# GpSimd's waits for free slots of gathered rows, moved from TensorE's products to the next step of ScalarE and VectorE, in a four-layer graph network

## The chip, the cores and the metric

The kernel runs on one core of a Trainium2 chip (trn2). The metric is the device time of one execution in microseconds (us): lower is better. The engines are TensorE (PE in the profile), VectorE (DVE), ScalarE (ACT), GpSimd (POOL) and SyncE (SP).

## The reference

A graph has 12,500 nodes of 64 features and 212,500 edges, sorted by their target node. Four layers run one after the other. Each normalizes the node features, makes a message for each edge from the row of its source node, adds the messages up by target and adds the result to the node features:

```python
# layer 0: softmax aggregation, feature by feature
m = relu(feats[src] + edge_h) + EPS
ex = exp(m - segment_max(m, dst)[dst]);  a = ex / segment_sum(ex, dst)[dst]
h = segment_sum(m * a, dst)              # then a norm, two matrix products and a batch norm
# layer 1: mean
agg = segment_sum(x[src], dst) / max(degree, 1);  out = concat([agg, x]) @ W.T + b
# layer 2: hyperbolic attention; u = -hh[row], v = hh[col] on the Poincare ball
ma = (coef1[:, None] * u + coef2[:, None] * v) / den[:, None]
e = -2.0 / sqrt_c0 * arctanh(clip(sqrt_c0 * norm(ma), 1e-08, CLIP))
att_log_h = segment_sum(softmax_over_row(e)[:, None] * log_h[col], row)
# layer 3: relational attention, 8 relations, 4 heads
s = leaky_relu(el[edge_rel, src] + er[edge_rel, dst]);  w = softmax_over_dst(s)
h = segment_sum(feat_all[edge_rel, src] * w[..., None], dst) + h_bias
```

## The kernel before

The program goes through nine stages. Each layer has one long loop over its edges, and a shorter stage follows each loop, in which the nodes are updated. The loops are `softmax_edges(0)`, `mean_edges`, `hyperbolic_edges` and `softmax_edges(3)`; the change touches only these.

**Steps and slots.** A softmax or mean loop has `STEPS` = 208 steps, each of two streams (`HALVES`) of `W` = 512 edges, in `TILES` = 4 tiles of 128. The hyperbolic loop has `CHB` = 230 steps of `BT` = 8 tiles of 128 edges. In each of the four loops GpSimd fetches the source rows of a step with eight indirect DMAs, one for each tile: lines 648 (both softmax loops), 955 (mean) and 1172 (hyperbolic). Rows land in a buffer of `SLOTS` = 4 slots (`rows`, in the profile `rows` or `m_rows`; `rows_d`, in the profile `h_rows_d`), so the gathers of step c overwrite the rows of step c - 4.

**The wait.** `slot_free(eng, sem, c, each, ago)` makes an engine wait until `sem` has reached `c * each + (1 - ago) * each`, that is until the step c - `ago` has been counted there; `each` is the number of increments in a step. It is nothing for the first `ago` steps:

```python
def slot_free(eng, sem, c, each=1, ago=2):
    if not (isinstance(c, int) and c < ago):
        eng.wait_ge(sem, c * each + (1 - ago) * each)
```

**Stages of a step.** Each engine executes its own list of stages, in program order. A stage with lag n works on the step that is n behind the newest one. The order of the lists sets the order of the work; no scheduler changes it.

- Softmax, layer 0. TensorE: `to_columns` (lag 0) turns the gathered rows and adds the edge features, in the product of line 765, whose last instruction increments `turned` (here `rows_read` is the same semaphore); then `count` (1) and `to_rows` (2). ScalarE: `move` (0, line 823, increments `moved`), `exps` (1, lines 827 and 828), `copy_out` (2, line 835), and a store. VectorE: bins (line 666), `segment_sums` (2), maxima (1, lines 698 to 706). SyncE's load of `attr` waits for `rows_read` too (line 614) and isn't changed.
- Softmax, layer 3. TensorE: `v_columns` (0), `score_columns` (1; line 787 increments `turned`), `to_rows` (3). ScalarE: `widen` (0), `move` (1, line 821, increments `moved`; it also waits until VectorE has bent the step before), then as above. VectorE: `own_values` (0, line 675), sums, maxima.
- Mean. TensorE: `to_columns` (line 966 increments `turned`), `to_rows` (line 973) and the products of line 985. VectorE's scan `segment_sums` (line 1048) waits for `turned` and increments `summed`. ScalarE copies out in line 1001.
- Hyperbolic. TensorE: `add_up` (3, line 1192, increments `multiplied`), `expand` (1, line 1210), `turn_hot` (0, line 1201, increments `turned`). ScalarE: square (2, line 1225), root, weigh, `move` (0, line 1234, waits for `turned`, increments `moved`). VectorE: `differ` (2), `messages` (3), `compare` (0), `distances` and `ratios` (2), and last `runs` (3, line 1338), eight operations of a chain that wait for `multiplied` and increment `ran` eight times in a step. In VectorE's turn `runs` stands behind `distances` and `ratios`, which need ScalarE's square and root.

Each of the later events is reached only when the earlier one has been, since `move`, `segment_sums` and `runs` wait for it.

Of the kernel before, what the change touches and what calls it, by code (L numbers as in the profile page):

```python
# [31 lines left out]
SLOTS = 4  # L32
# [15 lines left out]
BT = 8  # L48
# [28 lines left out]
def build(nc, x, src, dst, edge_attr, edge_type, w0a, b0a, gamma, beta, w0b, b0b, scale0,  # L77
          w1, b1, w2, c2, w3, al3, ar3, b3, out):
    with ExitStack() as whole:
# [30 lines left out]
        def counter(names, ctx):  # L110
            return [nc.alloc_semaphore(name=n) for n in names.split()]
# [274 lines left out]
        with nc.cleanup_on_exit(), ExitStack() as ctx:  # L386
# [8 lines left out]
            named, ran, prev_in, prev_out, normed, put, upto_ready, var_ready, std_ready = counter(  # L395
                "named ran prev_in prev_out normed put upto_ready var_ready std_ready", ctx)
# [126 lines left out]
# [4 lines that stand above are left out]
# [8 lines left out]
        def softmax_edges(layer):  # L535
# [6 lines left out]
            with nc.cleanup_on_exit(), ExitStack() as ctx:  # L542
# [6 lines left out]
                def sem(name):  # L549
                    return nc.alloc_semaphore(name=f"{name}_{layer}")  # L550
# [28 lines left out]
                if rel:  # L579
# [5 lines left out]
                    weighed, summed, back, copied, issue, pe_turn, got_b, parted, powered, merged, m_step, put_cross = (  # L585
                        sem(n) for n in (
                            "seeded v_turned v_spread v_own widened turned masked moved bent carried topped lowered diffed exped "
                            "weighed summed back copied issue pe_turn got_b parted powered merged m_step put_cross").split())
                scan_out = scan3 if rel else scan0
                ROWS = 16 * HALVES * TILES  # L590
                rows_read = turned
                END = (STEPS - 1) % 2

                with nc.Block() as block:
# [46 lines left out]
                    @block.gpsimd  # L641
                    def _(pool):
                        for c in range(STEPS):
                            b = c % SLOTS
                            slot_free(pool, rows_read, c, ago=SLOTS)
                            for k in range(TILES):
                                for h in range(HALVES):
                                    pool.indirect_dma_start(  # L648
                                        out=rows[:, b, k, h * GW:(h + 1) * GW], out_offset=None,
                                        in_=table3s.rearrange("n (q f) -> (n q) f", f=HEADS) if rel else table0,  # L650
                                        in_offset=bass.IndirectOffsetOnAxis(ap=idx_all[:, h, c, k:k + 1], axis=0)) \
                                        .then_inc(got_rows[b], 16)
# [199 lines left out]
        def mean_edges():  # L852

            with nc.cleanup_on_exit(), ExitStack() as ctx:
# [6 lines left out]
                def sem(name):  # L861
                    return nc.alloc_semaphore(name=f"m_{name}")
# [27 lines left out]
                seeded, turned, summed, back, copied, issue, blank, cleared, got_b, merged, put_cross = (sem(n) for n in (  # L890
                    "seeded turned summed back copied issue blank cleared got_b merged put_cross").split())
# [26 lines left out]
                with nc.Block() as block:  # L918
                    @block.sync
                    def _(sp):  # L920
                        def load(c, b, r):
                            slot_free(sp, summed, c, ago=SLOTS)
                            sp.sem_inc(issue, 1)
                            for h in range(HALVES):
                                sp.dma_start(same_b[h * D:(h + 1) * D, b, :],
                                             row(same, c + h * STEPS).broadcast_to([D, W])).then_inc(got_mask[b], 16)

                        def store(c, b, r):
                            sp.wait_ge(copied, c + 1)
                            sp.sem_inc(issue, 1)  # L930
                            for h in range(HALVES):
                                sp.dma_start(edge_rows(scan1, c + h * STEPS), out_e[:, b, h, :, :]).then_inc(put[b], 16)

                        steps(sp, STEPS, (0, load), (3, store))
                        for b in range(SLOTS):
                            sp.wait_ge(put[b], 32 * (STEPS // SLOTS))
                        last_b = sp.value_load(cross_i[0:1, 0:1], min_val=HALF, max_val=EP - 1)
                        sp.dma_start(state_b[:, 0:1], scan1[bass.ds(last_b, 1), :].rearrange("a f -> f a"),
                                     allow_slow_non_contiguous=True).then_inc(got_b, 16)
                        sp.wait_ge(merged, 1)  # L940
                        sp.dma_start(scan1[bass.ds(last_b, 1), :].rearrange("a f -> f a"), joined[:, 0:1],
                                     allow_slow_non_contiguous=True).then_inc(put_cross, 16)
                        sp.wait_ge(put_cross, 16)

                    @block.gpsimd
                    def _(pool):
                        pool.iota(columns[:, :], pattern=[[1, SORTED]], base=0, channel_multiplier=0,
                                  allow_small_or_imprecise_dtypes=True).then_inc(named, 1)

                        for c in range(STEPS):  # L950
                            b = c % SLOTS
                            slot_free(pool, turned, c, ago=SLOTS)
                            for k in range(TILES):
                                for h in range(HALVES):
                                    pool.indirect_dma_start(  # L955
                                        out=rows[:, b, k, h * D:(h + 1) * D], out_offset=None, in_=table1,
                                        in_offset=bass.IndirectOffsetOnAxis(ap=idx_all[:, h, c, k:k + 1], axis=0)) \
                                        .then_inc(got_rows[b], 16)
# [137 lines left out]
        def hyperbolic_edges(c_col, inv_sqrt_c):  # L1096

            with nc.cleanup_on_exit(), ExitStack() as ctx:
# [6 lines left out]
                def sem(name):  # L1105
                    return nc.alloc_semaphore(name=f"h_{name}")
# [26 lines left out]
                    weighed, messaged, multiplied, ran, u_step, c_turn, d_step, r_step, l_step, issue, issue_a, pe_turn = (sem(n) for n in (  # L1133
                        "upright got_map placed spread cleared split compared turned moved expanded apart squared spaced rooted bounded "
                        "weighed messaged multiplied ran u_step c_turn d_step r_step l_step issue issue_a pe_turn").split())
# [8 lines left out]
                with nc.Block() as block:  # L1144
                    @block.sync
                    def _(sp):
                        sp.dma_start(block_s[:, :], block_g.rearrange("(a n) -> a n", a=1)).then_inc(got_map, 16)
                        sp.dma_start(goes_on[:, :], goes_g.rearrange("(a n) -> a n", a=1).broadcast_to([P, NT])).then_inc(got_map, 16)
                        sp.wait_ge(got_map, 32)

                        def load_blocks(c, b, r):
                            slot_free(sp, expanded, c, ago=SLOTS)
                            sp.sem_inc(issue, 1)
                            _, blocks = nc.values_load_multi_w_load_instructions(
                                block_s[0:1, bass.ds(c * BT, BT)], engines=(mybir.EngineType.SP,), min_val=0, max_val=BLOCKS - 1)
                            for k, at in enumerate(blocks):
                                sp.dma_start(near[:, b, k, :], table2[bass.ds(at * P, P), 0:D + 1]).then_inc(got_near[b], 16)

                        steps(sp, CHB, (0, load_blocks))

                    @block.gpsimd
                    def _(pool):
                        pool.iota(place[:, :], pattern=[[1, P]], base=1, channel_multiplier=0,
                                  allow_small_or_imprecise_dtypes=True).then_inc(placed, 1)

                        for c in range(CHB):
                            b = c % SLOTS
                            if c * BT in (0, 8 * P):
                                pool.wait_ge(u_step, 3 + 3 * (c > 0))
                            slot_free(pool, multiplied, c, ago=SLOTS)  # L1170
                            for k in range(BT):
                                pool.indirect_dma_start(  # L1172
                                    out=rows_d[:, b, k, :], out_offset=None, in_=table2,
                                    in_offset=bass.IndirectOffsetOnAxis(ap=idx_d[:, c * BT + k:c * BT + k + 1], axis=0)).then_inc(got_rows[b], 16)
# [1033 lines left out]
```

## Time and profile before

| | |
|---|---|
| three runs | 12235.75, 12268.7 (median), 12348.68 us |
| the profiled execution | 12218.17 us, its span 12216.4 us |
| loop of layer 0 / mean / hyperbolic / layer 3 | 2507 / 2499 / 3152 / 2446 us |
| busy over the span: PE, DVE, ACT, POOL | 6560.5, 6951.0, 4184.0, 7235.6 us |

No engine is busy for more than 59% of the span. In the rows below, a line of a timeline has the start of an instruction (or of several merged, then with their number behind an x), its duration, its engine and line of the kernel, what it writes and reads, and in brackets how long the engine was idle just before it and what is thought to have ended that. The name behind such an arrow is inferred; where it names a DMA that landed long before, it was something else.

### The profile page before, as it was taken

What the parts mean: (1) busy time and instruction counts of PE and PEld (TensorE: products, weight loads), DVE (VectorE), ACT (ScalarE), POOL (GpSimd) and SP (SyncE); (2) the same over time, 40 slices, a digit from 0 to 9 for tenths busy, and PEclk for the clock granted to TensorE, in tenths of its full rate; (3) what the DMA queues carried; (4) which work ended last, traced back from release to release, by engine and by line L of the source; (5) the groups of instructions that cost most, each with busy time, mean ns of one, the idle gap of its engine ahead of it and who ended that gap; (6) DMA issues with size and microseconds to landing.
All of it is one profiled execution on the core that took longest, in us unless ns stands there. A gap on an engine that the chain in (4) does not pass through costs nothing. (4 is left out here: it accounts for less than half of the span.)

```text
span 12216.4 us, 120473 instructions
## 1 busy us (share of the span) xinstructions
PE 6560.5 (54%) x28159; PEld 5236.5 (43%) x28159; DVE 6951.0 (57%) x14143; ACT 4184.0 (34%) x8456; POOL 7235.6 (59%) x7482
## 2 busy tenths in 40 slices
PE   0655555553155555552356666666665555555552
PEld 0333333332145555551356666666664333333331
DVE  3556555667355555541645555555555477777775
ACT  0222222222055555551134444444444322222221
POOL 5666666664656666666155555555554666666665
PEclk9666666665577777775555555555556666666665
DMA  4333333332422222222033333333334444444442
GB/s 89 108 110 109 111 110 107 111 109 47 134 54 56 56 55 56 55 56 27 12 85 78 78 78 79 79 77 79 77 78 114 117 114 114 113 114 115 114 114 78
DMA packets 1318230, 1059.32 MB, mean 87 GB/s; under 512 B 815857, under 2 KB 1034376, under 8 KB 1316531
## 3 DMA queue, kind: packets, MB, share of 16 engines
q0 software_dynamic: 238720, 318.69, 13.9%
q1 hardware_dynamic: 681698, 373.56, 12.0%
q10 hardware_dynamic: 397397, 362.35, 9.1%
q8 instruction: 161, 2.64, 0.1%
q14 instruction: 254, 2.08, 0.1%
HBM read 580.99 MB, written 472.73 MB: 86 GB/s over the span
## 5 line engine op out<-in xcount | busy, mean ns | idle before, releaser
L1172 POOL DMA_INDIRECT h_rows_d<-table,h_idx_d x1840 | 1750.6, 951 | 1389.1 <-PE h_ps_sum L1192 812.6
L648 POOL DMA_INDIRECT rows<-table,idx_all x1664 | 1643.0, 987 | 870.8 <-issue 476.0
L955 POOL DMA_INDIRECT m_rows<-table,idx_all x1664 | 1575.0, 947 | 911.0 <-issue 453.2
L648 POOL DMA_INDIRECT rows<-table3s,idx_all x1664 | 1574.4, 946 | 872.5 <-issue 476.0
L985 PE MATMUL m_ps_sort<-m_hot_high,m_hot_low 128*128 128x224 f32 x3328 | 1056.9, 497 | 973.6 <-issue 818.2
L985 PEld LDWEIGHTS m_ps_sort<-m_hot_high,m_hot_low 128*128 128x128 f32 x3328 | 920.2, 283 | 1081.5 <-issue 941.0
L795 PE MATMUL ps_out<-ident,sums 128*128 128x128 f32 x3328 | 776.7, 398 | 965.6 <-issue 690.5
L1192 PE MATMUL h_ps_sum<-h_rows_d,h_hot 128*128 128x65 f32 x3680 | 832.0, 417 | 635.6 <-DVE h_rows_d L1329 352.1
L795 PEld LDWEIGHTS ps_out<-ident,sums 128*128 128x128 f32 x3328 | 629.9, 221 | 1131.5 <-issue 1075.6
L1192 PEld LDWEIGHTS h_ps_sum<-h_rows_d,h_hot 128*128 128x128 f32 x3680 | 795.4, 328 | 719.9 <-issue 719.9
L1210 PE MATMUL h_ps_src<-h_near,h_hot_t 128*128 128x65 f32 x3680 | 838.2, 419 | 462.1 <-DMA h_near<-table 252.8
L1210 PEld LDWEIGHTS h_ps_src<-h_near,h_hot_t 128*128 128x128 f32 x3680 | 803.1, 331 | 494.2 <-issue 493.6
L1048 DVE TENSOR_TENSOR_SCAN m_sums<-m_same_b,m_sums,m_ps_rows 128x512 f32<-128x512 bf16 x208 | 266.2, 1280 | 1078.5 <-issue 900.4
L835 ACT ACTIVATE out_e<-ps_out 128x512 f32<-128x512 f32 x832 | 446.3, 590 | 1049.3 <-remote 711.3
L1234 ACT ACTIVATE h_hot_t<-h_ps_hot 128x1024 f32<-128x1024 f32 x230 | 235.8, 1025 | 1566.2 <-DMA at_first<-m_zeros 1480.5
L666 DVE TENSOR_TENSOR hot<-bins,cat 128x784 bf16<-128x784 bf16 x208 | 202.8, 976 | 937.9 <-DMA rows_p<-dst_i,dest 847.1
L763 PE MATMUL ps_score<-ident,rows 128*128 128x128 f32 x1664 | 547.9, 423 | 305.4 <-issue 254.8
L1023 ACT ACTIVATE m_hot_low<-m_hot_low,record,m_slope 128x128 f32<-128x128 f32 x1664 | 663.8, 486 | 6.1
L1338 DVE SCALAR_TENSOR_TENSOR h_run<-h_run,h_goes_on,h_ps_sum 128x65 f32<-128x65 f32 x1840 | 519.2, 282 | 240.2 <-PE h_ps_sum L1192 6.2
L1087 DVE SCALAR_TENSOR_TENSOR m_junk<-cat,m_ps_base 128x98 f32<-128x98 f32 (+61 forms) x1664 | 594.2, 423 | 98.1 <-issue 50.6
L821 ACT ACTIVATE score_c<-ps_score 128x512 f32<-128x512 f32 x208 | 124.4, 598 | 1480.7 <-DMA table<-Hn 1196.5
L675 DVE TENSOR_TENSOR_SCAN spread_v<-marks,spread_v,ps_v 64x512 f32<-64x512 bf16 x208 | 263.7, 1268 | 635.9 <-issue 635.9
(425 smaller groups left out, 14233.0 us busy)
## 6 DMA issues: line engine op xcount, KB each, us to landing
scan<-out_e ACTq DMA_DIRECT2D x832, 256.0 KB
h_near<-table SPq DMA_DIRECT2D x1840, 32.5 KB
run_g<-h_run ACTq DMA_DIRECT2D x230, 260.0 KB
part_b<-part SPq DMA_DIRECT2D x832, 64.0 KB
max_b<-top ACTq DMA_DIRECT2D x416, 128.0 KB
scan<-m_out_e SPq DMA_DIRECT2D x416, 128.0 KB
attr<-in_edge_attr SPq DMA_DIRECT2D x415, 128.0 KB
h_rows_d<-table,h_idx_d POOLq DMA_INDIRECT x1840
```

The lines of the kernel that those rows point to most:

```text
L648: pool.indirect_dma_start(out=rows[:, b, k, h * GW:(h + 1) * GW], out_offset=None, in_=table3s.rearrange("n (q f) -> (n q) f", f=HEADS) if ...
L763: nc.tensor.matmul(ps_score[:, b % 2, k::TILES], rows[:, b, k, :], ident[:, :], start=True, stop=False)
L795: mm = nc.tensor.transpose(ps_out[:, j, k * P:(k + 1) * P], sums[:, b % 2, j, k::TILES], ident[:, :])
L835: ins = a.activation(out_e[:, b, :, :, j * D:(j + 1) * D], ps_out[:, j, :].rearrange("p (k h f) -> p h k f", k=TILES, h=HALVES), ACT.Copy)
L955: pool.indirect_dma_start(out=rows[:, b, k, h * D:(h + 1) * D], out_offset=None, in_=table1, in_offset=bass.IndirectOffsetOnAxis(ap=idx_al ...
L985: nc.tensor.matmul(ps_sort[:, 0:SORTED], hot_low[:, w % 2, j, :], hot_high[:, w % 2, j, :], start=n == 0, stop=n == PC - 1).then_inc(place ...
L1023: ins = a.activation(hot_low[:, w % 2, j, :], hot_low[:, w % 2, j, :], ACT.Relu, bias=record[:, at:at + 1], scale=slope[:, at:at + 1])
L1087: v.scalar_tensor_tensor(junk[:, at % 4, 0:BLOCKS + n], cat[:, p, 0:BLOCKS + n], cat[:, p, BLOCKS + n:BLOCKS + n + 1], ps_base[:, 0:BLOCKS ...
L1172: pool.indirect_dma_start(out=rows_d[:, b, k, :], out_offset=None, in_=table2, in_offset=bass.IndirectOffsetOnAxis(ap=idx_d[:, c * BT + k: ...
L1192: mm = nc.tensor.matmul(ps_sum[:, k // HB, (k % HB) * ACC2:(k % HB + 1) * ACC2], hot[:, b, k, :], rows_d[:, b, k, D + 1:ROW2], start=True, ...
L1210: mm = nc.tensor.matmul(ps_src[:, k // HB, (k % HB) * (D + 1):(k % HB + 1) * (D + 1)], hot_t[:, b % 2, k * P:(k + 1) * P], near[:, b, k, : ...
L1338: v.scalar_tensor_tensor(run[:, b, k, :], before, goes_on[:, bass.ds(c * BT + k, 1)], ps_sum[:, k // HB, (k % HB) * ACC2:(k % HB + 1) * AC ...
```

## The change

In each loop GpSimd's `slot_free` names another semaphore: in both softmax loops `moved` (ScalarE, lines 821 and 823) for `rows_read` (TensorE), in the mean loop `summed` (VectorE, line 1048) for `turned` (TensorE), in the hyperbolic loop `ran` (VectorE, line 1338, eight increments a step) for `multiplied` (TensorE). All are still four steps back. No instruction is added, removed or moved on any engine; the three lines below are all of it.

```diff
@@ softmax_edges, GpSimd @@
                             b = c % SLOTS
-                            slot_free(pool, rows_read, c, ago=SLOTS)
+                            slot_free(pool, moved, c, ago=SLOTS)
                             for k in range(TILES):
@@ mean_edges, GpSimd @@
                             b = c % SLOTS
-                            slot_free(pool, turned, c, ago=SLOTS)
+                            slot_free(pool, summed, c, ago=SLOTS)
                             for k in range(TILES):
@@ hyperbolic_edges, GpSimd @@
                                 pool.wait_ge(u_step, 3 + 3 * (c > 0))
-                            slot_free(pool, multiplied, c, ago=SLOTS)
+                            slot_free(pool, ran, c, each=BT, ago=SLOTS)
                             for k in range(BT):
```

## Rows read from the trace of the kernel before

**Rows 1.** Windows of the four loops: stretch and length, busy us (instructions), clock, DMA, GB/s

```profile
233.00:2740.00 2507.00, 1435.45 (x7018) 909.56 (x7019) 1464.85 (x1853) 545.45 (x1028) 1643.00 (x1664) 0.65 0.38 108
...
3046.00:5545.00 2499.00, 1259.84 (x4934) 1134.46 (x4934) 1261.11 (x3777) 1267.92 (x3520) 1575.34 (x1665) 0.74 0.26 66
...
6138.00:9290.00 3152.00, 2052.45 (x9184) 1936.06 (x9184) 1659.26 (x5280) 1412.33 (x1839) 1750.64 (x1840) 0.51 0.39 78
...
9564.00:12010.00 2446.00, 1376.87 (x5359) 944.84 (x5360) 1795.11 (x2260) 674.17 (x1441) 1574.41 (x1664) 0.64 0.41 112
```

**Rows 2.** Waits of GpSimd over the span: us in total, times, longest us

```profile
POOL h_rows_d L1172 <- PE h_ps_sum L1192: 812.6, 192, 11.8
...
POOL rows L648 <- DMA table<-Hn: 384.7, 102, 6.7
POOL rows L648 <- remote: 373.9, 102, 6.4
POOL m_rows L955 <- DMA rows<-table,idx_all: 293.3, 129, 10.3
...
POOL m_rows L955 <- PE m_ps_rows L966: 164.4, 58, 19.0
```

**Rows 3.** Timeline of the layer 0 loop, two steps

```profile
986.07 1.60 POOL L648 DMA_INDIRECT rows<-table,idx_all  x1 [3.64 <-remote]
...
998.95 0.44 PE L765 MATMUL ps_score<-ident,attr 128*64 128x128 f32 x4
...
1005.49 0.95 POOL L648 DMA_INDIRECT rows<-table,idx_all  x1 [0.30 <-issue]
...
1009.73 0.58 ACT L823 ACTIVATE ps_score<-ps_score 128x512 f32<-128x512 f32 x1 [2.62 <-remote]
...
1009.96 1.60 POOL L648 DMA_INDIRECT rows<-table,idx_all  x1 [3.53 <-remote]
```

**Rows 4.** Timeline of the layer 3 loop, the end of a batch of gathers

```profile
10507.42 0.95 POOL L648 DMA_INDIRECT rows<-table3s,idx_all  x1 [0.30 <-issue]
...
10512.01 0.60 ACT L821 ACTIVATE score_c<-ps_score 128x512 f32<-128x512 f32 x1 [11.77 <-DMA table<-Hn]
```

**Rows 5.** Timeline of the start of the layer 0 loop

```profile
282.68 0.95 POOL L648 DMA_INDIRECT rows<-table,idx_all  x1 [0.31 <-issue]
289.80 0.58 ACT L823 ACTIVATE ps_score<-ps_score 128x512 f32<-128x512 f32 x1 [24.10 <-remote]
```

**Rows 6.** Timeline of the stage behind the mean loop, ScalarE

```profile
5678.43 0.59 ACT L1427 ACTIVATE lin_rows_t<-lin_ps_t 128x500 f32<-128x500 f32 x1 [33.01 <-DMA m_same_b<-same]
```

**Rows 7.** Timeline of the mean loop, the end of a batch of gathers

```profile
4006.34 0.96 POOL L955 DMA_INDIRECT m_rows<-table,idx_all  x1 [0.30 <-issue]
...
4006.83 0.60 PE L966 MATMUL m_ps_rows<-ident,m_rows 128*128 128x128 f32 x4
...
4009.10 1.28 DVE L1048 TENSOR_TENSOR_SCAN m_sums<-m_same_b,m_sums,m_ps_rows 128x512 f32<-128x512 bf16 x1 [5.60 <-issue]
...
4009.28 0.95 POOL L955 DMA_INDIRECT m_rows<-table,idx_all  x1 [1.98 <-DMA rows<-table,idx_all]
```

**Rows 8.** Timeline of the hyperbolic loop, one step

```profile
7505.67 0.95 POOL L1172 DMA_INDIRECT h_rows_d<-table,h_idx_d  x1 [3.35 <-PE h_ps_sum L1192]
...
7508.82 3.19 DVE L1338 SCALAR_TENSOR_TENSOR h_run<-h_run,h_goes_on,h_ps_sum 128x65 f32<-128x65 f32 x8
...
7509.10 1.91 PE L1201 MATMUL h_ps_hot<-ident,h_hot 128*128 128x128 f32 x8
...
7513.54 3.65 PE L1192 MATMUL h_ps_sum<-h_rows_d,h_hot 128*128 128x65 f32 x16 [2.52 <-issue]
7514.43 0.95 POOL L1172 DMA_INDIRECT h_rows_d<-table,h_idx_d  x1 [0.30 <-issue]
7517.19 1.02 ACT L1234 ACTIVATE h_hot_t<-h_ps_hot 128x1024 f32<-128x1024 f32 x1 [6.51 <-DMA at_first<-m_zeros]
...
7517.60 0.95 POOL L1172 DMA_INDIRECT h_rows_d<-table,h_idx_d  x1 [2.22 <-PE h_ps_sum L1192]
...
7522.01 3.19 DVE L1338 SCALAR_TENSOR_TENSOR h_run<-h_run,h_goes_on,h_ps_sum 128x65 f32<-128x65 f32 x8
```

## The prediction, made before the changed kernel ran

> **What bounds the kernel now.** I first read the stage windows. In none of the four loops is an engine full: GpSimd, the busiest or nearly so, gathers for 1643 of 2507 us in layer 0, 1575 of 2499 in the mean loop, 1751 of 3152 in the hyperbolic one and 1574 of 2446 in layer 3 [rows 1]. A step takes 2507 / 208 = 12.05 us, 2499 / 208 = 12.01, 3152 / 230 = 13.70 and 2446 / 208 = 11.76. Eight gathers of 0.95 us with 0.30 us between them [rows 3] take 9.7 us of it. What is left is the time in which GpSimd waits for its slot, so these few microseconds are what the change works on. GpSimd's waits show them: 192 of 812.6 us in all before line 1172, 102 + 102 of 3.7 us before line 648 (every second step), 129 + 58 before line 955 [rows 2].
>
> Next I read timelines around such waits, for what GpSimd waits for and when it really was ready. Here is the odd thing. In layer 0 TensorE ends the last product of a step at 999.39, yet ScalarE's `move`, which waits for it, starts only at 1009.73, just when GpSimd starts again too, 3.3 us after the gather that ended at 1006.44 [rows 3]. In the mean loop the last gather ends at 4007.30, TensorE's product at 4007.43, and VectorE's scan and GpSimd both start at 4009.1 to 4009.3 [rows 7]. In the hyperbolic loop TensorE's `turn_hot` is over at 7511.01, the gathers at 7515.38, and ScalarE's `move` starts at 7517.19, GpSimd at 7517.60 [rows 8]. So work that TensorE has long finished reaches its waiters a fixed time behind the end of a batch of gathers: 1.8 us behind 8 gathers [rows 7, 8], 3.3 to 3.6 behind 16 [rows 3, 4], 6.2 behind the opening 40 [rows 5]. It grows with the batch. Behind the mean loop, where GpSimd issues 212 indirect DMAs and waits for none of TensorE's semaphores, ScalarE waits 33 us for a product [rows 6]: the gathers hold the news back, not GpSimd's own wait.
>
> The Trainium skill, Perfetto Trace Analysis, in "Tensor Engine Instruction", has the semaphore update pushed when PSUM acknowledges the last bytes, with no part in it for GpSimd. By that alone ScalarE would have started 10 us earlier in layer 0; the trace does not agree.
>
> What bounds a loop is then the cycle batch of gathers, hold, restart of GpSimd. Whatever delays the restart delays the next batch, its end, and the next release.
>
> **The change, part by part.** It adds no instruction. Queued behind the wait on GpSimd are only the gathers of this step and all later ones; TensorE (or ScalarE in layer 3) waits for these rows. SyncE's queue is passed by nothing, and its waits stay.
>
> *Do the rows come too late?* Between the release of step c - 4 and the use of step c lie about three periods, 36 us in the softmax and mean loops and 41 in the hyperbolic one; the gathers take 9.7 us. Some 24 us are spare, by this estimate. The added waits are 0.6, 1.3 and 6 to 8 us (below), so the rows still come in time and this costs nothing. The cover is thin only early in the mean loop, where GpSimd once waits 19.0 us [rows 2]: I allow 0 to 25 us for it and take 10.
>
> *Softmax, both layers.* At 1009.73 ScalarE starts `move`, and GpSimd now waits for its end, 0.58 us later, instead of starting at 1009.96. In layer 3 it is 0.60 us [rows 3, 4]. The wait bites once in two steps, 102 times a layer: 0.6 x 102 = 61 us in each, 122 us in all. Lower bound: 0, if the release of TensorE's news doesn't hang on the restart. Upper bound: every step pays, 0.6 x 208 x 2 = 250 us. I take 122, since the second step's `move` is done long before its eight gathers' turn.
>
> *Mean.* GpSimd starts 0.18 us after the scan has started; now it needs the scan's end, 1.28 us [rows 7]. 187 waits [rows 2] x 1.28 = 239 us. Bounds: 0 and 1.28 x 208 = 266. With the 10 us above: 249.
>
> *Hyperbolic.* This is the large unknown. Of the step whose `multiplied` lets GpSimd start at 7505.67, `runs` ends at 7512.01, 6.3 us later; of the next, at 7525.20 against 7517.60, 7.6 us later [rows 8]. If nothing overlapped, 6.5 x 226 = +1469 us would be the upper bound. But most of this lateness is VectorE standing behind `ratios`, work that goes on beside the gathers; with a later batch more of it is done when the release comes. What can't overlap is gathers 9.71, hold 1.81, the eight runs 3.19, restart 0.17: 14.88 us a step against 13.70. That is +1.18 x 226 = +267 us. Lower bound: the next two batches starting at 7505.67 and 7517.60 are 11.93 us apart [rows 8], which is a step whose wait is short; if the later start brought every step there, (11.93 - 13.70) x 230 = -407 us. I take +267, as it is the sum of the parts that stand in series in the trace.
>
> **Sum.** 122 + 249 + 267 = +638 us on the profiled execution's 12218.17: 12,856, forecast 12,850 us. That execution is 50.5 us (0.4%) under the median of 12268.7; against the median the forecast is +4.7%.
>
> **The rivals.**
>
> *Faster (opposite side).* The hold isn't uniform: `multiplied` of the product that ended at 7505.40 reached GpSimd at 7505.67, when no batch was running, and the later one of 7517.19 at 7517.60 [rows 8]. If the later restart puts TensorE's products into the pause between batches, their news comes at once, ScalarE and VectorE no longer wait for the end of a batch, and the chain gets shorter than the batch it waits for. For it speaks that GpSimd is idle more and the other engines are held less; against it, that a pause is only as long as the chain it waits for, and add_up (3.65 us) and the runs follow each other. It decides where `multiplied` is counted before the hold sets in. At the lower bound of the hyperbolic loop and no cost elsewhere: 12218 - 407 = 11,811; if the other loops still pay their 371, 12,182, within the measure of no change. Chance of a clear gain 0.13.
>
> *No change.* The news of TensorE is released by something that does not hang on when GpSimd restarts, and the spare 24 us swallow all. Then 12,218 to 12,243. For it: rows are fetched early. Against: three waiters on three engines start within 0.3 us of GpSimd [rows 3, 7, 8]. Chance 0.20, with the mixed case at 12,182. The rule of the Trainium skill quoted above (Perfetto Trace Analysis) belongs to this rival, since by it nothing ties a product's news to the gathers.
>
> *Only the small terms.* Hyperbolic breaks even, the rest pays: 12218 + 371 = 12,589. Chance 0.19.
>
> *No overlap.* The hyperbolic loop pays its lateness in every step, wholly or in large part: 12218 + 371 + 1469 = 14,058 at most, 13,200 if a third is paid. Chance 0.08.
>
> *It doesn't do what it says:* the new waits are reached before the old ones. It can't be, as each new event follows its old one.
>
> **How the numbers follow.** The forecast's own case has 0.40 and runs from 12,650 to 13,050 (softmax at 0 to 250, mean 239 to 291, hyperbolic 200 to 400). The range leaves out most of the clear gain and most of the no-overlap case, and holds the rest: 12,180 to 13,180. A measurement of this kernel can tell about 1%, 123 us, from no change: faster (under 12,146) 0.13, same 0.20, slower (over 12,391) 0.67, which is 0.40 + 0.19 + 0.08.
>
> **What the profile of after would show.** In layer 0, GpSimd's waits before line 648 go from 3.7 to 4.3 us, still every second step, and the loop from 2507 to about 2568 us. In the mean loop VectorE's scan still starts 1.8 us behind the last gather, GpSimd 1.3 to 1.5 us behind the scan, the loop takes about 2750. In the hyperbolic loop GpSimd waits 5.2 us before line 1172, nearly always for line 1338, and the loop takes about 3420 us. Gathers stay at 0.95 us, and the short stages stay as they are. I am wrong about the cycle if GpSimd's restart comes later and the loops don't get longer; wrong about the hold if the scan of the mean loop starts less than 1 us behind TensorE's product while gathers run; wrong about the overlap if line 1338 starts long after `multiplied` is counted.

## The result, and the profile after

The changed kernel takes 12838.78 us (median of three runs, 12832.34 to 12845.94) against 12268.7: ratio 1.0465, 95% interval 1.0433 to 1.0498. The forecast was 12,850. Its profiled execution took 12832.34 us, 614.2 more than that of before; the sum had said 638.

Where the time went is read from the page's costliest groups: line, engine, operation, count, busy us and mean ns of one, then the idle us just before them and what ended it. Busy and idle time of the gathers of one line together are the length of that loop's stream of gathers (with the idle time before its first gather). Before:

```profile
L1172 POOL DMA_INDIRECT h_rows_d<-table,h_idx_d x1840 | 1750.6, 951 | 1389.1 <-PE h_ps_sum L1192 812.6 <-issue 494.4 <-remote 73.3
L648 POOL DMA_INDIRECT rows<-table,idx_all x1664 | 1643.0, 987 | 870.8 <-issue 476.0 <-remote 373.9 <-POOLq L386 20.8
L955 POOL DMA_INDIRECT m_rows<-table,idx_all x1664 | 1575.0, 947 | 911.0 <-issue 453.2 <-DMA rows<-table,idx_all 293.3 <-PE m_ps_rows L966 164.4
L648 POOL DMA_INDIRECT rows<-table3s,idx_all x1664 | 1574.4, 946 | 872.5 <-issue 476.0 <-DMA table<-Hn 384.7 <-POOLq L1979 11.9
```

After:

```profile
L1172 POOL DMA_INDIRECT h_rows_d<-table,h_idx_d x1840 | 1747.1, 949 | 1762.7 <-DVE h_run L1338 1230.5 <-issue 524.1 <-DVE h_loc L1286 8.0
L955 POOL DMA_INDIRECT m_rows<-table,idx_all x1664 | 1575.8, 947 | 1072.6 <-DVE m_sums L1048 578.5 <-issue 473.3 <-DMA rows<-table,idx_all 20.8
L648 POOL DMA_INDIRECT rows<-table,idx_all x1664 | 1611.8, 969 | 945.1 <-issue 554.9 <-ACT ps_score L823 369.4 <-POOLq L386 20.8
L648 POOL DMA_INDIRECT rows<-table3s,idx_all x1664 | 1578.2, 948 | 904.8 <-issue 475.9 <-ACT score_c L821 417.0 <-POOLq L1979 11.9
```

| loop | stream before | after | difference | term of the sum |
|---|---|---|---|---|
| layer 0 | 2513.8 | 2556.9 | +43 | +61 |
| mean | 2486.0 | 2648.4 | +162 | +249 |
| hyperbolic | 3139.7 | 3509.8 | +370 | +267 |
| layer 3 | 2446.9 | 2483.0 | +36 | +61 |

The four differences are 611 of the 614 us. GpSimd's waits, which answer to [rows 2], now name the new semaphores' engines (us in total, times, longest us):

```profile
POOL h_rows_d L1172 <- DVE h_run L1338: 1230.5, 163, 15.8
...
POOL m_rows L955 <- DVE m_sums L1048: 578.5, 166, 7.4
...
POOL rows L648 <- ACT score_c L821: 417.0, 102, 6.8
POOL rows L648 <- ACT ps_score L823: 369.4, 85, 7.5
```

These rows don't hold every stop, since some are put down to other names. Counted in the two traces as gaps of over 0.4 us ahead of the first gather of a step, the stops are:

| loop | stops before | sum, us | stops after | sum, us |
|---|---|---|---|---|
| layer 0 | 102 | 373.9 | 147 | 460.3 |
| mean | 188 | 458.6 | 188 | 620.4 |
| hyperbolic | 226 | 885.8 | 179 | 1246.0 |
| layer 3 | 102 | 384.7 | 102 | 417.0 |

The timeline of the mean loop answers to [rows 7]: last gather, then TensorE's news, VectorE's scan, GpSimd.

```profile
4507.32 0.60 PE L966 MATMUL m_ps_rows<-ident,m_rows 128*128 128x128 f32 x4
...
4509.05 0.95 POOL L955 DMA_INDIRECT m_rows<-table,idx_all  x1 [0.30 <-issue]
4511.84 1.28 DVE L1048 TENSOR_TENSOR_SCAN m_sums<-m_same_b,m_sums,m_ps_rows 128x512 f32<-128x512 bf16 x1 [6.23 <-issue]
4513.39 0.95 POOL L955 DMA_INDIRECT m_rows<-table,idx_all  x1 [3.39 <-DVE m_sums L1048]
```

The scan still starts 1.84 us behind the last gather (4510.00), though TensorE was done at 4507.92, and GpSimd now starts 1.55 us behind the scan's start instead of 0.18: the stop of 1.98 us has become one of 3.39. This is the forecast's step, seen by itself: over the loop's 188 stops the median grew from 2.03 to 3.38 us. The traces also show that the rows came in time. From the end of the last gather of a step to the first use of its rows pass, in the median, 24.8 us in layer 0, 34.7 in the mean loop, 25.7 in the hyperbolic one and 14.9 in layer 3 before, and 28.6, 36.3, 24.7 and 14.5 after. A late row would be used at once, which is some 1.5 us behind its last gather (the shortest such time in these traces); after the change the rows of at most three steps of a loop were used within 2 us.

### The profile page after: what moved, and what is told of

The parts are those of the page before. It is cut to its first block and busy times, and to the rows that moved or that the text cites. A ratio compares the mean times of both kernels' runs of the same rounds, so it can differ in the third digit from the quotient of the medians.

```text
span 12830.6 us, 120473 instructions
## 1 busy us (share of the span) xinstructions
PE 6655.2 (52%) x28159; PEld 5300.2 (41%) x28159; DVE 6945.7 (54%) x14143; ACT 4178.9 (33%) x8456; POOL 7206.7 (56%) x7482
## 5 line engine op out<-in xcount | busy, mean ns | idle before, releaser
L648 POOL DMA_INDIRECT rows<-table,idx_all x1664 | 1611.8, 969 | 945.1 <-issue 554.9
L795 PE MATMUL ps_out<-ident,sums 128*128 128x128 f32 x3328 | 734.9, 390 | 525.2 <-ACT out_e L835 286.7
L763 PE MATMUL ps_score<-ident,rows 128*128 128x128 f32 x1664 | 634.4, 483 | 646.6 <-issue 596.8
L763 PEld LDWEIGHTS ps_score<-ident,rows 128*128 128x128 f32 x1664 | 402.8, 301 | 917.6 <-issue 917.6
```

What stands on the lines that cost most here:

```text
L648: pool.indirect_dma_start(out=rows[:, b, k, h * GW:(h + 1) * GW], out_offset=None, in_=table3s.rearrange("n (q f) -> (n q) f", f=HEADS) if ...
L763: nc.tensor.matmul(ps_score[:, b % 2, k::TILES], rows[:, b, k, :], ident[:, :], start=True, stop=False)
L795: mm = nc.tensor.transpose(ps_out[:, j, k * P:(k + 1) * P], sums[:, b % 2, j, k::TILES], ident[:, :])
```

## The experiments

The experiments ran in four groups, each on another chip, and the first group brought what I had not forecast: the kernel before took 10,076 us there, not 12,269. So it did, within 2 us, on three of the four chips. I call the late arrival of TensorE's news behind a batch of gathers the hold; on the fourth, with 12,001 us, the hold was there as in the first measurement. Each experiment below is told with the time of the kernel before on its own chip.

**The change without its hyperbolic part**:

```diff
-                            slot_free(pool, ran, c, each=BT, ago=SLOTS)
+                            slot_free(pool, multiplied, c, ago=SLOTS)
```

> The change without its hyperbolic part (that loop waits for multiplied again, the other three edits stay). The loops stand one after the other, so if each edit costs only in its own loop, the time is 12,839 less the 371 us by which the hyperbolic loop's gathers became longer: 12,468, with that loop's gathers back at 3131 us and the other three loops at their lengths in the changed kernel (2536, 2648, 2471 us). If instead the loops share a cause (for instance the clock), the hyperbolic loop stays above 3200 us.

Measured: 10078.26 against 10075.77 us, ratio 1.0002 (0.9993 to 1.0012). Neither 12,468 nor a price at all. The loops' edits could not be told apart where none costs anything.

**The first of the eight runs**, in the hyperbolic loop of the changed kernel:

```diff
-                            slot_free(pool, ran, c, each=BT, ago=SLOTS)
+                            if c >= SLOTS:
+                                pool.wait_ge(ran, (c - SLOTS) * BT + 1)
```

> The change, but in the hyperbolic loop GpSimd waits for the first of the eight increments of ran of step c - 4 (the other edits stay). It ends 7 x 0.4 = 2.8 us before the eighth. If the length of the eight runs is what costs, as my sum had it (3.19 of 3.19 us in series), GpSimd's 163 long waits shrink by 2.8 us each and the loop goes from 3502 to about 3050 to 3150 us, the time to 12,390 to 12,490. If what costs is that runs stands behind distances and ratios in VectorE's turn, the first run is as late as before and the loop stays above 3350 us (time above 12,690).

Measured: 10074.77, ratio 1.0000 (0.9990 to 1.0009). Nothing is paid here either, so it says nothing on the length or the place of `runs`.

**The change and the kernel before, again**, on another chip, to see whether the change itself costs nothing there:

> The change itself, all four loops, timed again. In the first four experiments the kernel before took 10,076 us, not 12,269, its gathers stood 1.25 us apart without a stop, and TensorE's news was prompt. If the hold behind gathers is what made the change cost 4.65%, then without a hold GpSimd never stops for a slot and the change costs nothing: 10,076 us within 0.2%. If the hold is there again on this chip, 12,839 against 12,269 again. A rival for the case without a hold: the hyperbolic loop, whose runs end 6 to 8 us behind multiplied, uses up the spare time of its rows and GpSimd stops now and then: 1 to 3 us in each of 226 steps, 10,300 to 10,750 us.

> The kernel before, profiled beside the change on the same chip. Without a hold: 1664 and 1840 gathers in a row without a stop in each loop, loops of 2131, 2078, 2326 and 2138 us of gathers, ScalarE's move in layer 0 within 0.3 us of the product's end. With the hold: 12,269 us and the loops of the first profile.

Measured: the change 10076.61 against 10075.85 us, ratio 1.0002 (0.9992 to 1.0012); the kernel before, profiled, 10066.36. The same program, the same instructions, 2200 us less. The page of the kernel before on this chip:

```profile
L1172 POOL DMA_INDIRECT h_rows_d<-table,h_idx_d x1840 | 1765.3, 959 | 569.5 <-issue 560.6 <-DVE h_loc L1286 8.9
L648 POOL DMA_INDIRECT rows<-table3s,idx_all x1664 | 1629.2, 979 | 518.3 <-issue 506.9 <-POOLq L1979 11.4
L648 POOL DMA_INDIRECT rows<-table,idx_all x1664 | 1620.7, 974 | 527.5 <-issue 506.9 <-POOLq L386 20.6
L955 POOL DMA_INDIRECT m_rows<-table,idx_all x1664 | 1571.5, 944 | 507.2 <-issue 507.2
```

The gathers last as long as ever, and nearly all idle time before them is the 0.30 us of issue: GpSimd never stops for a slot. Its timeline shows why.

```profile
1005.01 0.70 PE L765 MATMUL ps_score<-ident,attr 128*64 128x128 f32 x4
1005.75 0.58 ACT L823 ACTIVATE ps_score<-ps_score 128x512 f32<-128x512 f32 x1 [6.32 <-PE ps_score L765]
1006.23 0.94 POOL L648 DMA_INDIRECT rows<-table,idx_all  x1 [0.30 <-issue]
```

TensorE's product ends at 1005.71, ScalarE starts at 1005.75, in the middle of gathers that follow each other without end. In the first profile the same news took 10 us [rows 3]. It did so in every second step: of layer 0's 208 products 103 reached ScalarE late, by 10.3 us in the median, and the others within 0.05 us or so. On this chip all 208 did. So there is no hold here, GpSimd's gathers alone bound the loops (1.25 us each), and the change, which only delays a restart that never happens, is free. The spare time read from this trace, step by step, is 23.5 us for the old event and 22.9 for the new one in layer 0, 28.0 and 26.7 in the mean loop, 13.6 and 10.0 in the hyperbolic one, 25.5 and 18.1 in layer 3 (medians over all steps, from the end of the event's instruction to the gather that waits for it).

**`runs` ahead of `distances`** in VectorE's turn, with the change, on the chip of the first group, without the hold:

```diff
-steps(dve, CHB, (2, differ), (3, messages), (0, compare), (2, distances), (2, ratios), (3, runs))
+steps(dve, CHB, (2, differ), (3, messages), (0, compare), (3, runs), (2, distances), (2, ratios))
```

> The change, but VectorE's turn in the hyperbolic loop has runs ahead of distances and ratios. If the place in the turn is what costs, runs ends some 3.5 us behind multiplied and the loop gets to 14.9 us a step or less, 3300 us or less (time 12,640 or less). If the length of the runs is what costs, the loop stays at 3502 us within 50. If VectorE's chain of distances and ratios is itself what the loop waits for, putting 3.2 us ahead of it makes the loop longer than 3502 us.

Measured: 10726.31 against 10075.77, ratio 1.0647 (1.0629 to 1.0665). Its timeline, one step of 13.0 us:

```profile
6005.01 3.65 PE L1192 MATMUL h_ps_sum<-h_rows_d,h_hot 128*128 128x65 f32 x16 [4.25 <-DVE h_rows_d L1329]
...
6008.89 3.20 DVE L1338 SCALAR_TENSOR_TENSOR h_run<-h_run,h_goes_on,h_ps_sum 128x65 f32<-128x65 f32 x8 [2.93 <-PE h_ps_sum L1192]
6012.01 0.68 DVE L1310 TENSOR_REDUCE h_dist<-h_diff 128x8 f32<-128x512 f32 x1
6012.36 0.94 POOL L1172 DMA_INDIRECT h_rows_d<-table,h_idx_d  x1 [3.04 <-DVE h_run L1338]
```

It is nearest to the third of the outcomes, in that the loop got longer (its stream takes 2963 us against 2335 of the kernel before in the page above), but there the loop had not waited for `distances` and `ratios` at all. VectorE stands 2.93 us idle for the product of line 1192, time that `distances` and `ratios` had filled, and the step becomes a chain of 13.0 us which the gathers then have to wait for (221 stops, 661 us). The order of the kernel before was hiding add_up behind `distances`.

**A pause behind each gather**, in the kernel before, on the same chip:

```diff
+        def rest(pool, idle, n, sem, count):
+            pool.memset(idle[:, 0:n], 0.0).then_inc(sem, 1)
+            pool.wait_ge(sem, count)
...
                                         .then_inc(got_rows[b], 16)
+                                    rest(pool, idle, 1, rested, (c * TILES + k) * HALVES + h + 1)
```

> The kernel before, with a pause of some 0.2 us on GpSimd behind each gather of the four loops (a one-column memset and a wait for it), so that gathers stand about 1.5 us apart instead of 1.25. If the hold is a backlog that grows with each gather by about 0.2 us (1.8 us behind 8, 3.4 behind 16, 6.2 behind 40), this pace leaves no backlog: TensorE's news is prompt, ScalarE's move of layer 0 starts within 1 us of the product's end, and the steps settle at 12.0 to 12.5 us in all loops; that is nothing to +60 us in layer 0, the mean loop and layer 3 and 250 to 350 us less in the hyperbolic one: 11,950 to 12,150 us. If the hold is a fixed price of a batch and not a backlog, each step takes 1.5 to 2 us more: 854 steps, 13,500 to 13,900 us.

Measured: 10674.49 against 10075.77, ratio 1.0601 (1.0583 to 1.0619). The gathers start 1.33 us apart instead of 1.25; 600 us over 6832 gathers is 0.09 us each, so the pause is paid about one for one. It shows that the gathers bound the kernel there, and nothing about the backlog.

**The cover cut by two steps**, the kernel before and the change, `ago=2` in place of `ago=SLOTS` in GpSimd's four waits:

> The kernel before, with GpSimd's four waits set to the step c - 2 instead of c - 4 (its cover cut by two steps), on a chip without the hold. From the profile of the kernel before there, the old events are reached 2.9 us (layer 0), 8.1 (mean) and 5.0 (layer 3) before the gathers that would then wait for them, but multiplied 6.6 us after. So GpSimd never stops in three loops; in the hyperbolic one two steps take 26.8 us (from a gather's start to multiplied of that step, 4 x 10.1 - 13.6), 13.5 us a step against 10.1: +780 us, 10,860 us. If the rows were late anyway, all four loops get longer, by 3 us a step: +2600 us.

> The change, with its four waits set to the step c - 2. The new events are reached 2.3 us (layer 0) and 6.7 us (mean) before the gathers, but 2.4 us after in layer 3 and 10.2 us after in the hyperbolic loop. Where GpSimd has to stop, the lateness of the new event is paid, shared among the two steps: layer 3 (41 - 18.1) / 2 = 11.5 us a step against 10.25, +250 us; hyperbolic 30.4 / 2 = 15.2 us, +1170 us; the other two nothing: 11,500 us, 640 us over the one before. If a later event costs nothing as long as rows are fetched two steps ahead, both kernels with c - 2 are equal within 0.5%.

This chip had the hold: the kernel before took 12001.03 us, the median of seven runs between 11,820.61 and 12,014.62, a spread of 1.6% that stands behind every ratio of this group. Measured: 12932.6, ratio 1.0786 (1.0727 to 1.0844), and 14167.76, ratio 1.1822 (1.1758 to 1.1885). The pages, first of the kernel before so cut, then of the change:

```profile
L1172 POOL DMA_INDIRECT h_rows_d<-table,h_idx_d x1840 | 1740.4, 946 | 2194.8 <-PE h_ps_sum L1192 1691.1 <-issue 493.7 <-DVE h_loc L1286 10.0
L648 POOL DMA_INDIRECT rows<-table,idx_all x1664 | 1642.0, 987 | 852.3 <-issue 475.7 <-remote 355.8 <-POOLq L386 20.8
L648 POOL DMA_INDIRECT rows<-table3s,idx_all x1664 | 1600.2, 962 | 934.8 <-issue 471.7 <-PE ps_mult L787 232.5 <-DMA table<-Hn 219.1
L955 POOL DMA_INDIRECT m_rows<-table,idx_all x1664 | 1574.8, 946 | 880.4 <-issue 459.1 <-DMA rows<-table,idx_all 245.4 <-PE m_ps_rows L966 175.8
```

```profile
L1172 POOL DMA_INDIRECT h_rows_d<-table,h_idx_d x1840 | 1740.5, 946 | 2923.5 <-DVE h_run L1338 2420.8 <-issue 494.0 <-DVE h_loc L1286 8.8
L648 POOL DMA_INDIRECT rows<-table,idx_all x1664 | 1604.6, 964 | 962.4 <-issue 481.0 <-ACT ps_score L823 460.5 <-POOLq L386 20.9
L648 POOL DMA_INDIRECT rows<-table3s,idx_all x1664 | 1589.7, 955 | 1215.6 <-ACT score_c L821 757.0 <-issue 446.6 <-POOLq L1979 11.9
L955 POOL DMA_INDIRECT m_rows<-table,idx_all x1664 | 1575.8, 947 | 989.1 <-issue 518.0 <-DVE m_sums L1048 459.5 <-DMA rows<-table,idx_all 11.5
```

Two readings. With the hold, two steps less of cover hardly lengthen the streams of layer 0 (2494 us here against 2514 in the first profile) and of the mean loop (2455 against 2486), on a chip that is 2% faster for the whole kernel. So in these two loops the rows were not what was waited for, as the prediction said. In the other two the cut made them so: the rows of the hyperbolic loop are used 1.8 us behind their last gather in the median, those of layer 3 1.6, where it was 25.7 and 14.9 in the first profile. And the change costs, with the cover cut, by these streams, +73 us in layer 0, +110 in the mean loop, +729 in the hyperbolic and +270 in layer 3. Layer 3 and the hyperbolic loop, where the lateness of the new event is 7 us or so (25.5 - 18.1) and 3.6 to 7.6 us, pay the most once the cover is thin. This is the price of a later event where rows are already late, so it isn't the price that was forecast for four steps of cover. My expected sizes (0 in layer 0 and the mean loop, +390 in the hyperbolic one, +250 in layer 3) were for a chip without the hold; layer 3 came near, the others cost more.

**The hold put in by hand**, the kernel before and the change (`rest` as above). Each loop gets the pause, the count `news`, and a wait for it ahead of the first work that waits for TensorE; shown are GpSimd's part and the wait of the mean loop:

```diff
+                            for j in range(4):
+                                rest(pool, idle, 320, rested, 4 * c + j + 1)
+                            pool.sem_inc(news, SLOTS + 1 if c == STEPS - 1 else 1)
...
                             dve.wait_ge(turned, c + 1)
+                            dve.wait_ge(news, c + SLOTS)
```

> The kernel before with the hold put in by hand, for a chip that doesn't show it: behind each batch of eight gathers GpSimd pauses for 1.8 to 1.9 us (four memsets of 320 columns, each waited for) and then increments a semaphore news, and the first waiter for TensorE (ScalarE's move in the softmax loops, VectorE's scan of the mean loop and its eight runs in the hyperbolic loop) waits, besides for TensorE, until the batch of step c + 3 has been counted there, as it did in the first profile. GpSimd still waits for TensorE's event. Gathers 10.0 and pause 1.9 make 11.9 us a step in all loops, 854 steps x 1.9 = 1620 us more: 11,700 us.

> The change with the same hold by hand. Theory: what made the change cost time is that the work it waits for starts only when the hold ends, so its length stands in series with the gathers: +0.75 us a step in the softmax loops (150 us each), +1.45 in the mean loop (295), +3.4 in the hyperbolic one (770): 1365 us over the one before, 13,060 us. The rival, that the change cost time because rows came late or for a reason of its own in each loop, says the two held kernels are equal within 1%, since rows are fetched three steps ahead.

It ran on the chip that has the hold anyway, so the hold by hand came on top of the chip's own. Measured, against 12001.03 us: 12410.39, ratio 1.0312 (1.0223 to 1.0400), and 13066.51, ratio 1.0886 (1.0822 to 1.0951): the change costs 656 us, 5.3%, where TensorE's waiters are tied to the end of a batch by a semaphore too, and not by the chip alone. The second time is that of my forecast of 13,060, which is luck: it stood on 11,700 for the first. The pages, again of before and of the change:

```profile
L1194 POOL DMA_INDIRECT h_rows_d<-table,h_idx_d x1840 | 1761.7, 957 | 838.3 <-issue 514.6 <-PE h_ps_sum L1217 198.7 <-POOL h_idle L525 59.3
L656 POOL DMA_INDIRECT rows<-table,idx_all x1664 | 1654.0, 994 | 653.8 <-issue 500.4 <-POOL idle L525 132.6 <-POOLq L386 20.8
L656 POOL DMA_INDIRECT rows<-table3s,idx_all x1664 | 1624.6, 976 | 646.5 <-issue 474.5 <-POOL idle L525 159.3 <-POOLq L2005 12.7
L970 POOL DMA_INDIRECT m_rows<-table,idx_all x1664 | 1572.8, 945 | 658.1 <-issue 473.4 <-POOL m_idle L525 74.5 <-DMA rows<-table,idx_all 68.3
```

```profile
L1194 POOL DMA_INDIRECT h_rows_d<-table,h_idx_d x1840 | 1746.6, 949 | 1347.7 <-DVE h_run L1364 842.9 <-issue 493.3 <-DVE h_loc L1311 9.1
L656 POOL DMA_INDIRECT rows<-table3s,idx_all x1664 | 1587.1, 954 | 685.4 <-issue 466.5 <-ACT score_c L833 204.7 <-POOLq L2005 11.9
L656 POOL DMA_INDIRECT rows<-table,idx_all x1664 | 1576.8, 948 | 692.8 <-issue 466.4 <-ACT ps_score L835 203.1 <-POOLq L386 20.9
L970 POOL DMA_INDIRECT m_rows<-table,idx_all x1664 | 1573.4, 946 | 842.7 <-issue 452.2 <-DVE m_sums L1067 388.1 <-POOL m_idle L525 2.4
```

By loop +494 (hyperbolic), +185 (mean), -38 (layer 0) and +1 (layer 3). The change's timeline shows the hyperbolic loop in series, with the pause in it:

```profile
8013.38 1.65 POOL L525 MEMSET h_idle<- 128x320 f32 x4
...
8015.31 3.19 DVE L1364 SCALAR_TENSOR_TENSOR h_run<-h_run,h_goes_on,h_ps_sum 128x65 f32<-128x65 f32 x8 [6.07 <-POOLq L1199]
8018.78 0.95 POOL L1194 DMA_INDIRECT h_rows_d<-table,h_idx_d  x1 [3.75 <-DVE h_run L1364]
```

Pause, then the eight runs, then the next gather: this loop's steps are 15.2 us (8003.54 to 8018.78), the 14.88 of the prediction's sum within 0.4. Here the edit itself ties the runs to the pause, so this shows what such a series costs, not that the chip's hold makes one. The rival had said equal within 1%, but it had said so of a chip without the hold; on this one the change would have cost time by any cause, so the pair doesn't decide between them. What speaks against late rows are the 14 to 36 us between gather and use in the first two traces. My 1365 us was twice too high, as the two softmax loops paid nothing and the others two thirds.

**Once more**, the change without its hyperbolic part and the pause behind each gather, on a fourth chip. The hold was absent:

> The change without its hyperbolic part, once more, because the hold shows only on some chips (the kernel before takes about 12,000 to 12,270 us there and 10,076 us where it is absent). With the hold: the softmax and mean edits alone cost the 43 + 36 + 163 = 242 us by which these loops' gathers became longer, 2.0% over the kernel before of the same chip, and the hyperbolic loop's gathers take about 3130 us again. Without the hold: equal within 0.2%, as before.

> The kernel before with a one-column memset and a wait for it behind each gather, gathers about 1.33 us apart instead of 1.25 (measured on the chip without the hold, where it cost 600 us, as GpSimd's gathers bound the loops there). With the hold: if the hold is a backlog that grows by about 0.2 us a gather, 0.08 us more between gathers takes away 0.6 us of the 1.8 us behind eight, about what the pauses add, and the loops move by less than 100 us each except the hyperbolic one, where TensorE's news comes earlier: 50 to 200 us less; the whole 11,900 to 12,300 us where before takes 12,000 to 12,270. If the hold is a fixed price of each batch, each step takes 0.6 us more: +510 us.

Measured: 10076.92 against 10077.29, ratio 1.0001 (0.9992 to 1.0011), and 10676.84, ratio 1.0593 (1.0575 to 1.0610), as before. What the hyperbolic edit alone is worth with the hold, what the length and the place of `runs` are worth there, and whether slower gathers would undo the hold, was not seen. Nor was the plain change timed again on a chip with the hold: its 4.65% is that of the first measurement, and whether that ran on one of these four chips isn't known. No version beat the kernel before.

## Why the prediction was right, step by step

- **The bound: gathers, hold, restart.** Right where there is the hold. In both softmax loops GpSimd started 0.24 us behind the start of ScalarE's `move` before and 0.85 to 0.86 after, in the mean loop 0.18 us behind the scan's start before and 1.55 after (medians over the stops), and 611 of the 614 us are in the streams of gathers. With a hold by hand on top of the chip's own the change cost 5.3%. On a chip without the hold the kernel has another bound, the gathers alone, and there the change costs nothing (1.0002).
- **The rows come in time.** Right with the hold: the rows lay ready for 14 to 36 us in the median, and the streams of layer 0 and the mean loop hardly moved when two of the four steps of cover were taken away. The 10 us allowed for the thin start of the mean loop were not seen there: the stops of its first 26 steps sum to 39.3 us before and 40.4 after, though the rows of three of these steps were now used as soon as they had come. Without the hold the rows are used 1.5 to 2.2 us behind their last gather, so there the loops wait for rows in every step; what is spare is the time between the event and the gather that waits for it.
- **Softmax, 61 us each.** Measured +43 and +36. The delay of 0.6 us behind `move` was right, but the rest of the cycle didn't stay as it was. In layer 3 the stops are still 102, one in two steps, and grew from 3.77 to 4.09 us only, as `move` itself started 3.19 us behind the gathers' end instead of 3.63. In layer 0 the beat of every second step broke up: 102 stops of 3.7 us became 147 of 3.1. Why was not tested. The idle time before the gathers of layer 0 grew by 74 us, but their busy time fell by 31. A gather of 1.6 us stands at the start of a batch [rows 3]; 107 gathers of these two loops were longer than 1.2 us before and 73 after, and all but two of each lot ran beside VectorE's line 666, which starts at the same release. That a GpSimd that restarts later meets it less often fits this, but was not tested by itself. With the hold by hand the fall was 77 us, and layer 0 paid nothing. The Trainium skill, SBUF — State Buffer, in "SBUF: two separate sides", says that a VectorE operation with two SBUF inputs and a GpSimd operation that reads SBUF lock each other out of a shared port; line 666 reads `bins` and `cat` from SBUF. The trace agrees in part: before the change 299 gathers of layer 0 overlapped line 666, and 105 of them were long, all of which had started while it was already running.
- **Mean, 249 us.** Measured 162. The stop shown above grew by 1.41 us, a little more than my 1.28. But over all 188 stops the mean grew by 0.86 only, from 2.44 to 3.30 us, as the longest fell from 19.0 to 7.8. The mis-sized term is 187 waits x 1.28: as many waits, but not all of them paid it, and the allowance of 10 us came on top. Why some paid less was not tested.
- **Hyperbolic, 267 us.** Measured 370. The hold and the length of the runs were right, but that only the eight runs stand in series was not always so. The waits for TensorE's `multiplied` in [rows 2] were 192; with a further row the stops before the change were 226:

```profile
POOL h_rows_d L1172 <- remote: 73.3, 34, 2.2
```

  One step of the changed kernel:

```profile
8009.23 0.95 POOL L1172 DMA_INDIRECT h_rows_d<-table,h_idx_d  x1 [0.30 <-issue]
...
8012.56 0.17 DVE L1301 TENSOR_TENSOR h_prod<-h_ps_src,h_rows_d 128x8 f32<-128x8 f32 x1 [12.36 <-DMA max_b<-top]
...
8014.18 3.65 PE L1192 MATMUL h_ps_sum<-h_rows_d,h_hot 128*128 128x65 f32 x16 [14.05 <-DVE h_rows_d L1329]
...
8018.06 3.19 DVE L1338 SCALAR_TENSOR_TENSOR h_run<-h_run,h_goes_on,h_ps_sum 128x65 f32<-128x65 f32 x8
...
8021.52 0.95 POOL L1172 DMA_INDIRECT h_rows_d<-table,h_idx_d  x1 [11.35 <-DVE h_run L1338]
```

  The release (8012.56, 2.4 us behind the last gather) frees not the runs but `differ`, from which `messages`, add_up, `distances`, `ratios` and the runs follow: 8.7 us in series, a stop of 11.35. The runs of the next step were then done in time, so that 16 gathers followed without a stop, as they did 50 times in this loop and never before the change: 226 stops of 3.9 us in the mean became 179 of 7.0, and not the 5.2 us in nearly every step that I had forecast. That it isn't this step alone is seen from VectorE, whose idle time ahead of `differ` (line 1301, put down to a DMA) grew from 350.8 us in 90 waits to 1032.7 in 81. Why the loop fell into this pattern was not tested. The loop pays 1.6 us a step, between my 1.18 and the 6.5 of no overlap.
- **The sum** came out at 638 against 614 as its errors had both signs (43 us too much for softmax, 87 for the mean loop, 103 too little for the hyperbolic one). It was nearer than its terms deserve, and that is luck.
- **Slips in the working.** None of them moved the forecast. A third of the 1469 us would have given 13,079, not 13,200, and that lies inside the range. The forecast's own case, added up from its bounds, runs from 12,657 to 13,159, not to 13,050. And the waiters that start with GpSimd are on two engines, ScalarE and VectorE, within 0.41 us [rows 3, 7, 8].
- **The rivals.** That nothing would change came true only where there is no hold, and there for the rival's own reason, spare time. The faster case was not seen in any loop of the first measurement, though 50 batches of 16 gathers ran through without a stop. The case of no overlap would have been +1469 in the hyperbolic loop; 370 was seen.

What stays open: what makes the hold. The program and its data are the same with and without it, and a gather takes 0.94 to 0.99 us in the mean in either case; when the news arrives differs. It isn't TensorE alone that shows it: between the first and the last indirect DMA 603 of SyncE's 4930 MOVE, ALU_OP, SEQ_ASSERT and COMPARE_BRANCH instructions lasted over 0.5 us in the first profile, 548 of them while GpSimd's DMAs followed each other, and none of 4930 without the hold. ScalarE's news to VectorE (the exponentials, for line 712) came within 0.03 us in both. I didn't see what of a chip decides it.

## What to carry to other kernels

A semaphore wait that is four steps back is free only while its event is early; read from the trace when the waiter really starts, not only when the producer ends, since a late arrival of the news can put the next engine's work in series. Look which engine's restart closes the cycle, and leave its wait on the earliest event that makes the slot free. And time a kernel on more than one chip: the same edit cost 4.65% in the first measurement and nothing on another chip.

## What the runs showed of the hardware

- The same program took 12,269 us in the first measurement and 12,001, 10,076, 10,076 and 10,077 on four chips. TensorE's increments reached ScalarE 0.04 to 0.05 us behind the product on one chip. In the first profile about half of layer 0's did so and half took some 10 us; those that were late mostly came 1.8 us behind the last gather of a batch of eight (172 scans of the mean loop and 217 of the hyperbolic loop's `move`, medians 1.84 and 1.82) and 3.4 to 3.6 behind 16. After the change it was 2.1 us in the hyperbolic loop.
- A pause of 1.9 us by hand behind each batch cost only 3.1% on a chip with the hold, where 1.9 us a step would be 1620 us. The hyperbolic loop even took less, 2968 us from its first gather to its last against 3131 in the first profile, on a chip that is 2% faster. That pause and hold overlap is my reading; it wasn't tested.
- GpSimd's gather lasts 0.94 to 0.95 us, but 1.4 to 1.6, mostly 1.6, in 105 of the 299 that overlapped VectorE's line 666, which has two inputs in SBUF.
